# First layer's cross-attention: scores and values in pairs, reciprocals later, their product on GpSimd

## What is computed

```python
def sparse_norm(scores, nbias):
    t = jax.nn.relu(scores + nbias)
    t = t * t
    return t / (t.sum(-1, keepdims=True) + IEPS)
rq = (iQ @ Wq.T).reshape(b, q, h, a)
kv = iK @ Wkv.T
rk = kv[..., :hsize].reshape(b, s, h, a)
rv = kv[..., hsize:].reshape(b, s, h, a)
scores = jnp.einsum('bqha,bsha->bhqs', rq, rk) / np.float32(np.sqrt(a))
scores = jnp.where(mask[:, None, :, :], jnp.float32(MASK_FILL), scores)
attn = sparse_norm(scores, nbias)
o = jnp.einsum('bhqs,bsha->bqha', attn, rv).reshape(b, q, hsize)
return o @ Wo.T
```

## Time and profile before

| what | us |
|---|---|
| median of 3 runs | 2936.61 |
| lowest, highest | 2935.52, 2940.99 |
| the profiled execution | 2925.96 |
| its span | 2924.1 |
| TensorE busy | 2613.8 |
| VectorE busy | 1442.7 |
| ScalarE busy | 1088.5 |
| GpSimd busy | 681.2 |

### The profile page before, as it was taken

One profiled execution on the slowest core, in us unless ns is written; L12 is line 12 of the kernel. 1 busy time (PEld: TensorE's weight loads), 2 busy tenths in 40 slices (PEclk: granted clock), 3 DMA queues, 4 the chain that ended last, 5 costly groups with the idle time before them and its releaser, 6 DMA issues. The chain is left out here.

```text
span 2924.1 us, 40088 instructions
## 1 busy us (share of the span) xinstructions
PE 2613.8 (89%) x16441; PEld 1564.8 (54%) x16441; DVE 1442.7 (49%) x2107; ACT 1088.5 (37%) x1885; POOL 681.2 (23%) x364
## 2 busy tenths in 40 slices
PE   7679999989999999999949978999989998699997
PEld 4256533844266534754228855464554544477776
DVE  5566337932876347932821124555445554633432
ACT  3764234722564245622502213534335342011111
POOL 0256024900665034900720020000000000022222
PEclk9889999999999999999979987999999998699999
DMA  5550002100030002100039940010100102144442
GB/s 198 200 186 25 0 1 98 60 1 1 1 134 23 1 0 111 46 1 0 1 133 329 343 144 16 1 23 23 22 23 1 23 8 94 34 146 147 166 164 73
DMA packets 62126, 219.25 MB, mean 75 GB/s; under 512 B 12293, under 2 KB 28122, under 8 KB 45178
## 3 DMA queue, kind: packets, MB, share of 16 engines
q1 hardware_dynamic: 45802, 187.39, 17.7%
q0 software_dynamic: 9568, 18.75, 2.7%
q10 hardware_dynamic: 6576, 10.57, 1.0%
HBM read 172.50 MB, written 39.99 MB: 73 GB/s over the span
## 5 line engine op out<-in xcount | busy, mean ns | idle before, releaser
L652 PE MATMUL psum<-arena 128*128 128x256 f32 (+7 forms) x4224 | 1098.4, 411 | 66.4 <-ACT arena L1514 11.5
L652 PEld LDWEIGHTS psum<-arena 128*128 128x128 f32 (+1 forms) x4224 | 679.0, 196 | 434.9 <-issue 321.1
L2473 POOL TENSOR_TENSOR arena<-arena 128x1024 f32<-128x1024 f32 x128 | 299.5, 2372 | 98.4 <-DVE arena L1979 83.5
L1979 DVE TENSOR_TENSOR_SCAN arena<-arena,psum 128x512 f32<-128x512 f32 x256 | 290.8, 1200 | 22.4 <-PE psum L793 14.6
L793 PEld LDWEIGHTS psum<-arena 128*128 128x128 f32 x2048 | 236.6, 193 | 49.4 <-ACT arena L1544 40.3
L793 PE MATMUL psum<-arena 128*128 128x128 f32 x2048 | 249.0, 279 | 2.0 <-issue 1.9
L2508 POOL DMA_INDIRECT arena<-xn,arena x32 | 31.6, 987 | 859.3 <-DVE arena L2415 807.6
L2480 POOL TENSOR_TENSOR arena<-arena 128x1024 f32<-128x1024 f32 x32 | 75.9, 2373 | 653.0 <-ACT arena L1632 653.0
L2073 DVE SCALAR_TENSOR_TENSOR arena<-psum,arena 128x1024 f32<-128x1024 f32 x128 | 156.8, 1243 | 80.5 <-PE psum L938 80.1
L1632 ACT ACTIVATE arena<-arena 128x1024 f32<-128x1024 f32 x128 | 146.7, 1146 | 110.1 <-DVE arena L2073 109.9
L1811 ACT ACTIVATE arena<-psum 128x256 f32<-128x256 f32 x128 | 49.2, 384 | 322.1 <-PE psum L652 322.1
(11 more groups left out here) (293 smaller groups left out, 2985.3 us busy)
## 6 DMA issues: line engine op xcount, KB each, us to landing
arena<-in_W SPq DMA_DIRECT2D x46, 1024.0 KB
arena<-c_rows SPq DMA_DIRECT2D x32, 512.0 KB, 3.9
arena<-in_Wg SPq DMA_DIRECT2D x16, 1024.0 KB, 4.9
arena<-in_Wu SPq DMA_DIRECT2D x16, 1024.0 KB, 7.6
arena<-in_Wd SPq DMA_DIRECT2D x16, 1024.0 KB, 10.0
arena<-in_xT SPq DMA_DIRECT2D x8, 512.0 KB, 5.9
zs_all<-arena SPq DMA_DIRECT2D x4, 1024.0 KB, 3.9
ut_all<-arena SPq DMA_DIRECT2D x4, 1024.0 KB, 8.8
```

The source lines that it names most:

```text
L652: r = mm(dst, w, x, start=i == 0, stop=i == len(pairs) - 1)
L1979: V.tensor_tensor_scan(hs[n % 3][:, c, :], dA[n % 2][:, c, :], bank[4 + c], 0.0, ALU.mult, ALU.add)\
L2473: nc.gpsimd.tensor_tensor(h, h, c_all[:, n % CBUFS, :].unsqueeze(1).broadcast_to([P, 2, L]), ALU.mult)\
```

## The change

The TensorE loop issues two score units, then two value units, and `sum_weights(hp - 1)` comes behind the first two value units of pair hp. VectorE takes the reciprocals of pair hp - 2 behind the first and the third relu of pair hp, and no longer multiplies in the loop. GpSimd does that product for pair hp - 2 between its second and third addition of pair hp, for the first six pairs; VectorE still does the last two behind the loop, after a wait that keeps the count of `xo_ready` in order.

```diff
--- before.py
+++ after.py
@@ -959,14 +959,16 @@
                         i = mm(bank[1][64 * r:64 * r + 64, :], ones1[:, 0:64], tsum[hp % 2][:, r, :], start=True, stop=True)
                     i.then_inc(den_full.sem, 1)
 
-                for u in range(SBUFS):
-                    xscores(u)
-                for u in range(UX):
+                xscores(0)
+                xscores(1)
+                for u in range(0, UX, 2):
+                    if u + 2 < UX:
+                        xscores(u + 2)
+                        xscores(u + 3)
                     weigh_values(u)
-                    if u % NC == 1 and u > NC:
+                    weigh_values(u + 1)
+                    if u % NC == 0 and u > 0:
                         sum_weights(u // NC - 1)
-                    if u + SBUFS < UX:
-                        xscores(u + SBUFS)
                 w(t_ready, UX)
                 tiles = [LV.fill(pe, b, "xo", m) for m in range(KD)]
                 for k in range(8):
@@ -2072,13 +2074,11 @@
                     t = psum[:, 2 + 2 * (u % SBUFS):4 + 2 * (u % SBUFS), :]
                     V.scalar_tensor_tensor(rl[u % RBUFS], t, minus_nb8, bound[:, kc, :].unsqueeze(1).broadcast_to([P, 2, L]),
                                            ALU.max, ALU.min).then_inc(relu_done.sem, 1)
-                    if kc == 3 and hp >= 1:
-                        invert_sums(hp - 1, 0)
-                    if kc == 0 and hp >= 2:
-                        invert_sums(hp - 2, 1)
-                    if kc == 1 and hp >= 2:
-                        heads_out(hp - 2)
+                    if kc % 2 == 0 and hp >= 2:
+                        invert_sums(hp - 2, kc // 2)
+                invert_sums(HP - 2, 0)
                 invert_sums(HP - 2, 1)
+                w(xo_ready, HP - 2)
                 heads_out(HP - 2)
                 invert_sums(HP - 1, 0)
                 invert_sums(HP - 1, 1)
@@ -2482,6 +2482,11 @@
                         pool.wait_ge(t_ready.sem, t_ready.at(NC * hp + kc + 1, b))
                         pool.wait_ge(tsum_step.sem, tsum_step.at((NC - 1) * hp + kc - 1, b))
                         nc.gpsimd.tensor_tensor(t, t, t2[kc], ALU.add).then_inc(tsum_step.sem, 1)
+                        if kc == 2 and hp >= 2:
+                            pool.wait_ge(den_inv.sem, den_inv.at(2 * (hp - 1), b))
+                            pool.wait_ge(od_kept.sem, od_kept.at(3 * (hp - 2) + 1, b))
+                            nc.gpsimd.tensor_tensor(xqT[:, hp - 2, :], o_raw[hp % 2], den[hp % 2], ALU.mult)\
+                                .then_inc(xo_ready.sem, 1)
             pool.wait_ge(rd_a.sem, rd_a.at(0, 1))
             pool.wait_ge(stored_zero.sem, 16)
             pool.wait_ge(ld_x0.sem, 16)
```

## The result

The changed kernel takes 2904.27 us in the median, against 2936.07 us for the kernel before; the ratio is 0.9883 with a 95% interval of 0.9859 to 0.9906. The profiled execution took 2905.99 us, its span 2903.8 us. I had forecast 2901.9 us. A second, later set of the same two kernels gave 2906.74 against 2934.65 us, ratio 0.9896 (0.9877 to 0.9914). Medians and ratios leave out two executions that took several times as long as all others, 7428.70 us of the kernel with TensorE's order alone and 14289.22 us of the kernel before; nothing is read from them. Each set has its own executions of the kernel before, with medians from 2933.93 to 2936.07.

A forecast was written before the change was run, and what follows sets the result against it. TensorE was taken to bound the loop's 9.61 us period to within half a microsecond. Four loops saving 8.68 each, 34.7 in all, off the median of 2936.61 gave 2901.9 us, range 2891 to 2914.

The forecast's parts named there:

- The sum: Whole forecast for the first layer's cross-attention pair loop: 76.63 to 67.95 us, 8.68 saved per loop, 34.7 over four loops.
- head: Start of the pair loop, from its first score unit until the steady period begins: predicted to end at 9.71 us.
- six slots: Steady periods of the pair loop, each one pair of heads (four score units, four value units, one weight sum): 8.44 us each.
- the last slot: Final pair of heads in the loop, no scores after its first pair, last value unit waiting for its square: 7.6 us.
- The tail: Work behind the loop: two more VectorE reciprocals and a product delayed by GpSimd's last addition stay hidden under TensorE, costing nothing.
- Pairs: TensorE in the loop: two score units take 1.92 us, two value units 1.87, so 8.44 per pair of heads against 9.14.
- Product on GpSimd: Product moved to GpSimd in the loop: 1.27 us, upper bound 1.72; GpSimd's list 8.41 per pair of heads.
- The estimate of 1.35: GpSimd's product in the loop priced from the skill page, 1.96 x 0.69 = 1.35 us; period 8.49, about 1 us over four loops.
- the 0.36 on the accumulator drain: TensorE wait in the old loop: a value unit 0.36 us late, released by the old accumulator's drain; predicted to go.
- Part 2: Reciprocals taken later on VectorE in the loop: same count, no wait before them, list 7.94 us, 0.5 to spare.
- level of 10.65: Whole-kernel time: the median of the runs taken as 10.65 us above the profiled execution's 2925.96, giving 2936.61.
- its own case: Main forecast for the whole kernel: saving 31 to 36 us, 2900 to 2906 from the median, chance 0.80.

## Why the prediction was right

**The sum.** Predicted 34.7 us, 8.68 a loop; the traces show 8.63 a loop and 34.5. Its terms held, in the third loop: head 9.76 us (9.71 forecast), six slots of 8.43 (8.44), the last slot 7.63 (7.6), in which the last value unit waits 1.05 for its square as worked out. The tail is free, as forecast, though VectorE's product took 2.69.

**Pairs.** Entering and leaving costs of 0.05 and 0.10 per group came out of the earlier trace rows and held to 0.01: 1.91 to 1.92 for two score units, 1.87 for two value units.

**Product on GpSimd.** 1.27 was taken between 1.26 and 1.72, and 1.26 to 1.29 is what 24 products took. The reason stood too: neither relu nor reciprocal holds it. Behind that sentence the Trainium skill (SBUF — State Buffer, Who interferes with whom) has it that only a VectorE instruction with two SBUF inputs or in a two-port mode contends with GpSimd. The runs agree, 1.27 beside reciprocals, and 2.80 for VectorE's own two-input product beside an addition. The estimate of 1.35 that the prediction worked out from the ratio 1.96 of the Trainium skill (GPSIMD Engine Reference, Elementwise — side-by-side cycle accounting) was 0.08 too high: measured here, the ratio is 1.27 / 0.69 = 1.84. At 8.49 the slot would have been longer than it is.

**The step that failed: what bounded the kernel before.** The prediction had "TensorE therefore bounds the slot to within half a microsecond", took the 0.36 on the accumulator drain and 0.11 "spread over the others" for the rest of 9.61 (the 0.11 is one wait, of the second value unit for its square), and costed Part 2 only by its room on VectorE. The runs show otherwise. The slot was the circle of waits through sum product, drain, both reciprocals, two relus, a square and a value unit, 9.61 by itself, and TensorE's waits were its shadow. By the prediction's terms the pairs alone would have given 0.7 a slot; they gave 0.00. The reciprocals' delay, which it priced at nothing, is what had to come first: put back, it costs 1.18 a slot. The sum came out because all three parts were made together and the circle was gone, and because the prediction had checked every wait of the new slot. For the cause of the old slot this was luck: a forecast for one part by the same reading would have been wrong by some 20 us, since pairs alone came to 1.6 a loop, where 0.7 a slot and the 0.36 make 7.

**Size against the median.** With a level of 10.65 over the profiled execution, the forecast is the median of the kernel before less 34.7: 2901.9, and 2904.27 was measured. Both sets of runs give less than the traces' 34.5 us (31.8 and 27.9). Their intervals hold it, but the second lies below the saving of 31 to 36 that the prediction gave its own case; scatter outside the loops was not in that window.

## What to carry to other kernels

Before pricing an engine's list, look for a circle: start at a wait that recurs each period, follow the releasers until the same instruction comes back, and add the steps. If the sum is the period, work off the circle does not count, however full its engine is, and the cure is to use a result later than it comes. Here that cost no time and no new buffer, because the sums already had two. With the circle gone the longest list sets the period: 9.14 with TensorE's old order, 8.43 with the pairs. Work that goes to another engine needs the room there, and work that stays may meet collisions; count both.

## What the runs showed of the hardware

- A VectorE product with two SBUF inputs beside a GpSimd addition took 2.80 us instead of 0.69, and the pair of GpSimd additions 5.14 instead of 4.87. The product ended 0.53 to 0.55 behind the end of the addition that it met, whether it had started 0.08 behind that addition's start (2.83), 0.21 (2.69), or 1.1 (1.79, before the change), as if it waited for the whole of it. Relus with one input in PSUM took 1.18 to 1.29 and reciprocals 1.69 to 1.76 in both kernels, and GpSimd's product beside them 1.26 to 1.29.
- On TensorE, going from 64-row products to 64-column products and back costs 0.35 us a pass (2.07 for a score unit and a value unit in turn, against 2 x 0.86). Two passes less a slot gave 0.71 (9.14 to 8.43).
- A period can be the same to the hundredth (9.61) in three kernels whose lists differ by 0.7 us on TensorE, 0.6 on VectorE and 1.2 on GpSimd.
